# A graph network on one core: groups of cells two places later, and the degree factor as a power on GpSimd

## The reference

```python
# layer 0: gated GCN, four gates
x1 = h @ W1 + b1                                   # 1250 x 512
deg = segment_sum(ones, dst); dis = max(deg, 1) ** -0.5
for k in range(4):
    alpha = tanh(out[dst] @ gw[:512] + out[src] @ gw[512:] + gb)
    out = out + segment_sum(dis[src] * dis[dst] * alpha * out[src], dst)
x = x + concat(x1, out)
# layer 1: x + h @ W.T + bias, W a 1024 x 1024 matrix summed up from edge_weight at (src, dst)
# layer 2: GCN with self loops, norm (deg + 1) ** -0.5, then ReLU
# layer 3: graph attention: exp(-leaky_relu(al[src] + ar[dst])), weighted mean, ELU
```

## Time and profile before

| | us |
|---|---|
| median of 3 runs | 1001.96 (1000.94 to 1003.04) |
| profiled execution | 1001.58 |
| its span | 1000.0 |
| PE busy | 977.4 |
| DVE busy | 668.7 |
| ACT busy | 430.9 |
| POOL busy | 140.4 |
| PE waits for DVE's cells (L1822), ACT's cells (L1822) | 1.7, 0.7 |

### The profile page before, as it was taken

One profiled execution on the slowest core, in us unless ns is written; L12 is line 12 of the kernel. 1 busy time (PEld: TensorE's weight loads), 2 busy tenths in 40 slices (PEclk: granted clock), 3 DMA queues, 4 the chain that ended last, 5 costly groups with the idle time before them and its releaser, 6 DMA issues.

```text
span 1000.0 us, 14720 instructions
## 1 busy us (share of the span) xinstructions
PE 977.4 (98%) x5170; PEld 809.6 (81%) x5170; DVE 668.7 (67%) x1221; ACT 430.9 (43%) x650; POOL 140.4 (14%) x191
## 2 busy tenths in 40 slices
PE   5999999999999999999999999999999999999997
PEld 3788788888888888888888888888888888888886
DVE  7877888788778879354485343216446664988886
ACT  5688865554543646112242322233222232445543
POOL 3022500000000010232221000000110000333331
PEclk9999999999999999999999999999999999999999
DMA  7256580000000014745433111243451230101223
GB/s 251 101 177 222 136 255 1 1 22 0 0 21 0 0 12 104 178 171 188 180 124 116 42 42 43 77 155 106 156 180 69 69 121 0 43 22 64 84 84 122
DMA packets 27326, 93.42 MB, mean 93 GB/s; under 512 B 3530, under 2 KB 3530, under 8 KB 27136
## 3 DMA queue, kind: packets, MB, share of 16 engines
q1 hardware_dynamic: 16400, 58.07, 16.5%
q0 software_dynamic: 10880, 34.74, 11.4%
HBM read 64.48 MB, written 33.56 MB: 98 GB/s over the span
## 4 chain that ended last, share of the span: by engine, by line
PE 91%; DVE 5%; ACT 2%; issue 1%; POOL 1%; DMA 0%; ACTq 0%; DVEq 0%; POOLq 0%
PE ps L592 32%; PE ps L2052 11%; PE ps L1972 9%; PE ps L1974 9%; PE ps L1973 9%; PE ps L2025 5%; PE ps L2024 5%; PE ps L575 3%; PE ps L1895 1%; PE ps L1897 1%; PE ps L1896 1%; PE ps L1866 1%; PE ps L1822 1%; PE ps L1825 1%; PE ps L1838 1%
## 5 line engine op out<-in xcount | busy, mean ns | idle before, releaser
L1972 PE MATMUL ps<-g_hi,mask_hi 128*128 128x512 f32 x400 | 157.4, 394 | 2.1 <-DVE mask_lo L1513 2.1
L1974 PE MATMUL ps<-g_hi,mask_lo 128*128 128x512 f32 x400 | 155.9, 390 | 0.0
L1973 PE MATMUL ps<-g_lo,mask_hi 128*128 128x512 f32 x400 | 155.7, 389 | 0.0
L558 ACT ACTIVATE hT_hi<-ps 128x1024 fp32r<-128x1024 f32 x40 | 41.0, 1025 | 200.3 <-PE ps L575 200.3
L592 PE MATMUL ps<-w_hi,hT_hi 128*128 128x512 f32 x320 | 126.4, 395 | 0.0
L592 PE MATMUL ps<-w_lo,hT_hi 128*128 128x512 f32 x320 | 124.7, 390 | 0.0
L2052 PE MATMUL ps<-y_all,att_hi 128*128 128x512 f32 x400 | 110.0, 393 | 1.5 <-DVE att_lo L1693 1.5
L1110 ACT ACTIVATE mask<-ps,v 128x640 f32<-128x640 f32 x80 | 63.4, 793 | 111.2 <-PE ps L1974 52.9
L592 PE MATMUL ps<-w_hi,hT_lo 128*128 128x512 f32 x320 | 98.6, 389 | 0.0
L1972 PEld LDWEIGHTS ps<-g_hi,mask_hi 128*128 128x128 f32 x400 | 75.1, 188 | 20.4 <-DVE mask_lo L1513 3.3
L2052 PEld LDWEIGHTS ps<-y_all,att_hi 128*128 128x128 f32 x400 | 74.0, 188 | 17.3 <-DVE att_lo L1693 1.5
(11 more groups left out here) (203 smaller groups left out, 1839.2 us busy)
## 6 DMA issues: line engine op xcount, KB each, us to landing
xin<-x_after SPq DMA_DIRECT2D x30, 512.0 KB, 3.3
xres<-x_after POOLq DMA_DIRECT2D x20, 512.0 KB, 4.2
x_after<-xres POOLq DMA_DIRECT2D x20, 512.0 KB, 3.0
w_raw<-in_L_gnn_W SPq DMA_DIRECT2D x8, 1024.0 KB, 7.2
x_after<-g POOLq DMA_DIRECT2D x20, 256.0 KB, 7.4
xres<-x_after SPq DMA_DIRECT2D x10, 512.0 KB, 3.4
xin<-in_x SPq DMA_DIRECT2D x9, 512.0 KB, 3.4
out_x<-xres SPq DMA_DIRECT2D x9, 512.0 KB, 2.7
```

The source lines that it names most:

```text
L1972: nc.tensor.matmul(SUMS[dd], mask_hi[k][:, cols], g_hi[:, s, :], start=(s == 0), stop=False)
L1973: nc.tensor.matmul(SUMS[dd], mask_hi[k][:, cols], g_lo[:, s, :], start=False, stop=False)
L1974: last = nc.tensor.matmul(SUMS[dd], mask_lo[k][:, cols], g_hi[:, s, :], start=False, stop=(s == T - 1))
```

## The change

The groups move two places later in all three lists (SHIFT). POOL splits the edge weights ahead of the first scale, and SCALES_AHEAD is new. The first bias moves from k=2 to k=6 of ACT's weight split. The degree factor comes from a power on POOL in place of the square root and reciprocal; POOL does it after its count stores and ahead of its additions to x1. The one-element tanh goes to the end of step 8, in the last step ACT takes the product of tile 8 ahead of the last counts, and the second tanh stands ahead of the wait for dis. take_x1 of the last tile and the third tanh change places with mask_hi. DVE's gates 3, 4 and 5 each stand later or earlier by some places. In the last attention group both elu_end come after the last step, and ACT has two waits for them ahead of its next takes.

```diff
+SHIFT = 2
-SCALES_AHEAD = {0: 1, 1: 2, 4: 3, 7: 4}
+SCALES_AHEAD = {0: (1, 2), 3: (3,), 7: (4,)}
     def groups_at(t, place, lead):
-        g = PER_STEP * (t - FIRST_STEP) + place + lead
+        g = PER_STEP * (t - FIRST_STEP) + place - SHIFT + lead
     def tiles_behind(t, place, behind):
-        g = PER_STEP * (t - FIRST_STEP) + place - behind
+        g = PER_STEP * (t - FIRST_STEP) + place - SHIFT - behind
# POOL
-        pool.wait_ge(firsts_done, 1)
-        scale_pool(pool, 0)
         pool.wait_ge(ew_landed, 16)
...
         nc.gpsimd.tensor_copy(part[2], left_over[1]).then_inc(parts_chain, 1)
+        pool.wait_ge(firsts_done, 1)
+        scale_pool(pool, 0)
         for a in range(T):
-            if a in SCALES_AHEAD:
-                scale_pool(pool, SCALES_AHEAD[a])
+            for i in SCALES_AHEAD.get(a, ()):
+                scale_pool(pool, i)
...
         pool.sem_inc(built, 1)
+        pool.wait_ge(norm_chain, 2)
+        nc.gpsimd.tensor_tensor(dis[:, :, :], norm[:, :, :], minus_half[:, 0:1].unsqueeze(2).to_broadcast([P, 2, T]),
+                                ALU.pow).then_inc(norm_power_ready, 1)
# ACT
         for k in range(KT):
-            if k == 2:
+            if k == 6:
                 place_bias(0)
...
-            place_act(t, 0)
+            if t < T - 1:
+                place_act(t, 0)
             if t > 0:
                 take_x1(t - 1)
+            if t == T - 1:
+                place_act(t, 0)
...
             place_act(t, 3)
+            if t == T - 2:
+                nc.scalar.activation(rden[:, 0, 1:2], zeros[:, 0:1], ACT.Tanh).then_inc(tanh_idle, 1)
...
-        act.wait_ge(norm_chain, 2)
-        nc.scalar.activation(norm_root[:, :, :], norm[:, :, :], ACT.Sqrt).then_inc(norm_root_ready, 1)
-        nc.scalar.activation(rden[:, 0, 0:1], zeros[:, 0:1], ACT.Tanh).then_inc(tanh_idle, 1)
...
         tanh(0, 0, 0, 0)
+        act.wait_ge(count_stored[0], 16 * HT)
+        tanh(0, 0, 0, 1)
         act.wait_ge(dis_ready, 1)
         act.wait_ge(product_read[0], 1)
         g_split(0)
-        act.wait_ge(count_stored[0], 16 * HT)
-        tanh(0, 0, 0, 1)
         mask_hi_of(0, 0)
         act.wait_ge(product_read[1], 1)
         g_split(1)
+        take_x1(T - 1)
+        mask_hi_of(0, 1)
         act.wait_ge(product_ready[0], HT)
         tanh(0, 0, 0, 2)
-        take_x1(T - 1)
-        mask_hi_of(0, 1)
...
+        act.wait_ge(gat_added, T - GRP - 1)
         gat_take(T - 2, 0)
         elu_act(T - 2, 0)
+        act.wait_ge(gat_added, T - GRP)
         gat_take(T - 1, 1, slice(0, HID))
# DVE: gates(3, 3) moves from behind place 1 to ahead of place 2 of step 8, gates(4, 4) behind
# place 2, gates(5, 5) behind place 3 (it stood behind the Newton step)
-        dve.wait_ge(norm_root_ready, 1)
-        nc.vector.reciprocal(dis[:, :, :], norm_root[:, :, :]).then_inc(norm_chain, 1)
+        dve.wait_ge(norm_power_ready, 1)
...
-                if not first and s in (7, 8):
+                if not first and not last and s in (7, 8):
                     elu_end(GRP * (grp - 1) + s - 7, grp - 1, s - 7)
+            if last:
+                for j in range(GRP):
+                    elu_end(GRP * (grp - 1) + j, grp - 1, j)
```

More of the change, by code:

```diff
@@ L371, in build_program @@
     norm_chain = sem("norm_chain")
-    norm_root_ready = sem("norm_root_ready")
+    norm_power_ready = sem("norm_power_ready")
     tanh_idle = sem("tanh_idle")
@@ L1417, in _ @@
             place_dve(t, 1)
-            if t == T - 2:
-                gates(3, 3)
             if t + 2 < T:
@@ L1437, in _ @@
             if t == T - 2:
+                gates(3, 3)
+            place_dve(t, 2)
+            if t == T - 2:
                 gates(4, 4)
-            place_dve(t, 2)
             place_dve(t, 3)
+            if t == T - 2:
+                gates(5, 5)
             if t == T - 3:
```

9 lines of the change are left out of this document (3 added, 6 removed).

## The result

The changed kernel took 1006.92 us in the median of 5 runs (1006.20 to 1008.02), the kernel before 1001.96 (1000.94 to 1003.04): a ratio of 1.0048, 95% interval 1.0036 to 1.0059. It is slower by 0.48%, clear of the 0.2% that a measurement can tell, and outside the range given. The profiled execution took 1008.02, its span 1006.5; the profiled one of before had 1001.58 and 1000.0.

A forecast was written before the change was run, and what follows sets the result against it. PE, busy 98% of the span, was taken as the bound, so only its waits could shrink. Terms 2.5 + 0.1 + 0.4 - 0.2 - 0.85 - 0.5 - 0.4 gave 1.05 us faster than 1001.96: 1000.9, range 997.6 to 1005.6.

The forecast's parts named there:

- head, kept at tile 3: Kernel start: earlier edge-weight split starts tile 0's product 2.9 us sooner, of which 2.5 us remains at tile 3's transposes.
- stand in step 2: Step t=2: the 1.7 us wait for DVE's cells goes, a new 1.7 behind ACT's queue comes; net gain 0.1.
- stand at 69.30: PE's 0.7 us wait where row copy, ReLU and bias precede one group: gain 0.4, bounds 0 and 0.7.
- steps 7 and 8: Step before the last: three groups and two row copies come close, ACT's copy of group 23 ends late; loss 0.2.
- clock: PE's clock falling after standing idle: 0 in the main sum; after 6.5 us of standing, 2.4 us more, chance 0.03.
- gate: Start of the first gated aggregation: PE starts 8.4 us + p after the last count transposes begin; loss p + 0.1, 0.85.
- behind the gate: Four steps after the gate: DVE sets the pace and the third g_lo comes 0.6 later; loss 0.5, bounds 0 and 1.
- tail: Kernel end: PE loses its att_lo wait, but the output buffer's store and reload chain comes late; loss 0.4, not gain 1.3.
- rival 1: Gate: power grows with columns, p = 5.4, total 1005.6, or 1008.0 with lower clock; decides from p = 3.8; chance 0.24.
- p: Time of POOL's degree-factor power on 20 columns at the gate, taken as 0.75 us, at least 0.7, 5.4 if per column.
- Rival 2: Step 2 and tail: the new waits do not form, total 997.6, about 998.9 with either alone; chance 0.34.

The follow-up runs named there:

- run 12: Changed kernel, with POOL's last cast of the head made to wait for DVE's first weight split: 1007.45 us, ratio 1.0061 to the kernel before.
- run 7: Changed kernel with its tail undone, both ELU ends ahead of the last att_lo again and no ACT waits: 1006.62 us, ratio 1.0056 to the kernel before.
- run 9: Kernel before, plus scratch powers, multiplications and twelve casts in POOL's idle time in the first gated stage: 1001.0 us in one run.
- run 1: Changed kernel with the head's old order back, scale ahead of edge-weight split and first bias at k=2: 1005.80 us, ratio 1.0041 to the kernel before.
- run 6: Kernel before, with only POOL's 20-column power in place of the square root and reciprocal: 1003.16 us, ratio 1.0015.
- Run 10: Changed kernel with early degree factor, scale of tiles 8 and 9 one place earlier, step 2's group 0 copy ahead of ReLU and bias: 998.54 us, ratio 0.9969.
- Run 5: Changed kernel with POOL's scale of tiles 8 and 9 one place earlier in its queue: 1004.95 us, ratio 1.0034 to the kernel before.
- run 14: Kernel of run 11 plus a separate, early-loaded buffer for the last tile's residual: 998.30 us, ratio 0.9966 to the kernel before.
- run 3: Changed kernel with the power in two instructions of 10 columns, only the first refined ahead of the first mask: 1004.38 us, ratio 1.0024.
- run 16: Kernel of run 11 with the tail as before the change: 998.46 us, ratio 0.9966 to the kernel before.
- run 11: Kernel of run 10, with the head's last cast waiting for DVE's first weight split: 998.30 us, ratio 0.9967 to the kernel before.
- run 15: Kernel of run 14 plus a separate early-loaded buffer for tile 8's residual: 997.37 us, ratio 0.9957 to the kernel before.

## Why the prediction was wrong

In the profiled pair, gain (-) or loss (+) in us; stands are taken from matmul start to matmul start, less 0.23:

| step | forecast | found | from |
|---|---|---|---|
| head, kept at tile 3 | -2.5 | +0.7 | 33.33 to 34.02 |
| stand in step 2 | -0.1 | -0.4 | 1.9 to 1.5 |
| stand at 69.30 | -0.4 | -0.6 | 0.9 to 0.3, at 104.04 |
| steps 7 and 8 | +0.2 | +1.9 | 1.5 at 109.06, 0.4 behind it |
| clock | 0 | +1.4 | 15.73 to 17.14, see above |
| gate | +0.85 | +2.3 | 1.0 to 3.3 |
| behind the gate | +0.5 | +0.5 | +5.84 to +6.33 |
| tail | +0.4 | +0.2 | +6.33 to +6.53 |
| sum | -1.05 | +6.0 | the span: +6.5; 0.5 has no place |

**The head failed most, at "begun at 10.1, before DVE, the whole split [...] needs 2.8 and ends at 12.9".** It was to bring 2.5 us and cost 0.7 in this pair. The split did begin at 10.46, and DVE's own began at 12.80, ahead of that end. I had the row that warned of it, the same cast at 0.39 and at 2.00, and took it as a price for being late, not as one that a shorter overlap could raise to 3.93. The rest of the step was right in kind: where the cast was quick (10 of 14 profiles with this order), tile 1's transposes started at 16.2 to 17.5, where I had 16.2. But "kept: 2.5" was too much there too: at tile 3 run 12 had gained 0.5 against before and run 7, the quickest, 1.3. And the scale behind the split was not free: in the slow case the bias came at 18.94 and held ACT's list.

How much of the head is chance shows where one order was profiled several times. With the old order tile 3's transposes started at 33.33 (before), 32.77 (run 9), 33.89 (run 1) and 34.68 (run 6). With the changed order they started at 32.05 to 32.97 in the ten quick profiles and at 33.65 to 34.51 in the four slow ones. So the 0.7 of one pair is within the spread of a single order. With the quick cast the change brought 0.4 to 1.3 us against the kernel before, not 2.5, and the slow cast took it back.

**The waits of step 2 and near 69 us were right in kind and size.** ACT's queue (ReLU, bias, copy) took the place of DVE's cells, 1.3 us at 41.5 where I had 1.7 at 37, so only its place was off. Run 10 removed it by the order of that queue.

**Steps 7 and 8 were missed, at "In the step before the last, three groups and two row copies come close together", priced at -0.2.** I followed ACT's row copies and not the entry between them, the bias of tile 8, whose scale POOL computes behind its own stores. I named POOL's queue as one to be walked through for the gate and did not walk through it here. Five of its six small operations took 0.62 to 0.97 us beside DVE, where those of rows 7 take 0.19 and 0.71. Run 5 shows that one place in that queue was worth the stand and what followed.

**The clock was priced only inside rival 1**, for a stand of 6.5 us, at 0.03. It fell behind a stand of 1.4 and cost as much again.

**At the gate the term p was mis-sized**: 3.55 us instead of 0.75. My ground was that POOL's casts hardly grow with columns; a cast says nothing of a power. The two bounds, 0.7 and 5.4, held it. Of the step's other terms the degrees came 2.1 after the transposes, not 3.4, because the load that I had put in ACT's queue did not exist: tanh's load in the kernel before had followed the square root's, and without a square root the changed kernel loads no table between its copies, its ReLUs and the tanh. The power started 3.5 after the transposes instead of 4.9, so the loss was 2.3 instead of the 3.65 that 3.55 makes in my formula.

The Trainium skill, page "GPSIMD Engine Reference", section "Performance versus the Vector engine", has 2.6 cycles per element for a two-input operation, by which I let the sum stay. Run 9 comes near it for the multiplication (0.48 us on 20 columns, 0.64 on 80: 3.2 cycles of 1.2 GHz per column) and not for the power, 0.160 us per column or 190 such cycles: the rule does not cover a power, and I used it as if it did.

**Behind the gate and in the tail** the steps held to 0.2 us: the DMA chain took over, with store and reload of 4.8 us (992.37 to 997.17) as in the forecast. Where I had said that one faster store would bring nearly all of the 1.3, run 14 corrects it: both buffers have to be free.

**The rivals.** Rival 1 had the right side and one of the causes, a power that grows with its columns. That its 1005.6 and the 1008.0 with a lower clock enclose the 1006.92 is luck: with p = 3.55 its sum gives 1000.9 + 2.8 = 1003.7, below its own decision point (p from 3.8 on), and the other 3.2 us come, as far as the profiles tell, from the head, steps 7 and 8 and a clock that fell at another place. Run 6 prices the power at 1.0 to 1.5 us in the old order. Rival 2's condition, new waits that do not form, did not come.

## What to carry to other kernels

A bound that comes from another operation (a cast's growth for a power's) is no bound: with 0.7 and 5.4 as the only ends, the chance belongs between them. When groups of work are moved, list every queue entry between two uses of the moved work, on each engine, with what it waits for; here the costly one was a bias of 0.7 us waiting for six tiny operations on another engine. Work on the last critical path is cheapest where most of its input is known earlier: eight of ten columns of the degree factor could be computed ahead, and the power then cost 0.4 instead of 3.2 us of waiting.

## What the runs showed of the hardware

**POOL beside DVE.** The cast of 80x250 took 0.39 us alone and 0.71 to 0.74 beside DVE's splits (0.74 to 0.87 beside DVE in run 9), 2.00 and 1.67 in the heads of the kernel before and of run 1, and 3.93, 4.20, 4.11 and 3.12 in four changed heads (the changed kernel, runs 3, 5 and 16). These four began at 12.81, 12.50, 12.62 and 13.56 and all ended within 0.1 of 16.7, 0.24 us behind the end of DVE's sixth split, with which DVE paused; DVE's splits kept their 0.68 us. The ten quick ones (0.71 to 0.74) began at 12.89 to 14.13, and a split beside them took 0.8 to 1.0. So one engine pays or the other. What decides is open: begun at 13.56 and at 13.62, each 0.22 behind the start of a split, the same cast went both ways. The Trainium skill, page "GPSIMD Engine Reference", section "Specifications", says that the two engines share their SBUF interfaces and contend, among other cases, where DVE's instruction has two SBUF inputs. The trace agrees as far as it goes: the weight split has two such inputs, and the cast of 0.39 at 11.66 ran beside an operation that reads one of its inputs from the tensor memory (L565, 11.67). In the slow cases one engine was held off for 3 to 4 us, over five or six instructions of the other.

**The clock behind a short stand.** Of 14 profiles with a stand over 1 us behind the head, 6 have the clock at 1.2 GHz for a while afterwards (3.4 us in five, 6.8 in run 5): behind 1.4 us twice, 2.5 once and 3.2 three times; behind three more stands of 3.2 and 3.3 it stayed up. None of the four profiles without such a stand has it before PE's last matmul. A fall cost 0.8 to 2.1 us here, in the changed kernel as much as the stand ahead of it. The spread of the times does not tell the kernels apart: 0.6 to 2.4 us in the kernels of runs 10, 11 and 14 to 16, 1.8 in the changed one, 4.4 in run 12. What makes it fall in one run and not in the next is open.
